# Graph attention on one core: value products on alternate column halves, and the denominators and degrees on four column groups of a bank of their own

## The chip, the cores and the metric

The kernel runs on one core of one Trainium2 chip. The metric is the device time of one execution in microseconds (us); lower is better.

## The reference, cut to what matters

Four graph layers run one after the other over 6,250 nodes of 64 features and 206,250 edges. Only the first, the attention layer, is touched by the change:

```python
def _L0_gnn_ref(x, edge_index, qk_w, qk_b, v_w, v_b, o_w, o_b, ln_g, ln_b):
    qk = x @ qk_w.T + qk_b
    v = x @ v_w.T + v_b
    src = edge_index[0]
    dst = edge_index[1]
    scores = jnp.sum(qk[dst] * qk[src], axis=-1) / math.sqrt(v.shape[-1])
    scores = jnp.clip(scores, -5.0, 5.0)
    seg_max = jax.ops.segment_max(scores, dst, num_segments=n)
    e = jnp.exp(scores - seg_max[dst])
    seg_sum = jax.ops.segment_sum(e, dst, num_segments=n)
    attn = e / seg_sum[dst]
    out = jax.ops.segment_sum(attn[:, None] * v[src], dst, num_segments=n)
    ...
```

The second layer needs the degree of each node, the number of edges that end in it, and takes it from the same pass.

## The kernel before, in words

The edges have been turned into a dense matrix of counts in DRAM (float16: how many edges lead from one node to another). The attention layer goes over this matrix as a dense one. Its columns, the receiving nodes, are cut into 13 **bands** (`NGRP`): the first, n = 0, has 352 columns (`GCOLS`, the last 128 nodes and 224 overflow columns), the other twelve 512. Its rows, the sending nodes, are 49 blocks of 128 (`NB`). One **iteration** i = 49 n + hi is one block of one band:

- `score(i)` (TensorE, L1185): the 128 x 512 scores, from 64 rows of `qT`, float32. Even iterations use array rows 0 to 63, odd ones rows 64 to 127. There are four banks for scores (`SB`, banks 0 to 3).
- `exp(i)` (ScalarE, L873): the exponential into `expo`, eight buffers (`EB`).
- `clip(i)` (VectorE, L1889) limits it to exp(-5) and exp(5), and `weigh_(i)` (VectorE, L1901) multiplies it by the counts in `chunkA` into `weighed`, eight buffers (`WB`). VectorE's order is written out: clip(i) always stands ahead of weigh_(i - 1), and at the end of a band too.
- `gain(i)` (TensorE, L1194): `vtab` times `weighed`, float32, added up over the 49 blocks in bank 4 or 5 (`SB + n % AB`). `vtab` has 66 columns: 64 values, a column of ones, whose product is the denominator (`seg_sum`), and a column of zeros.
- `degree(i)` (TensorE, L1202): 32 columns of `degw` times the counts themselves (float16) into the same bank, rows 64 to 95 and 96 to 127 in turn, which gives the degrees.

TensorE's order is written out as well, in **groups** of four iterations (`QUAD`): the scores of a group, then the gains and the degrees of the group before it, then what `between` adds. A band is twelve full groups and one of a single iteration (hi = 48):

```python
                    for i in now:
                        score(i)
                    for i in before_:
                        gain(i)
                    for i in before_:
                        degree(i)
                    for i in before_:
                        between(i)
                    before_ = now
```

`between` holds what belongs to a band's end. `att_fold(n)` (L1213) adds the overflow columns to a finished band with two products of 256 columns. ScalarE's `att_out(n)` (L881) copies the bank to `outT`. `att_back(n)` (L1222), at block 8 of the next band, turns it back to rows of nodes with four products against `mergeA` in bank 6, and VectorE's `att_sum` copies them to `sumsA`. Once, in band 1, the overflow columns are turned in the same way (L888, L1232, L1931).

SyncE loads `chunkA`, a ring of two buffers (`ARING`), four chunks to a band (`UCH`): three of 14 blocks (`CCH`) and one of 7. A load waits until the degrees of the chunk before the last are done (`att["used"]`).

Of the kernel before, what the change touches and what calls it, by code (L numbers as in the profile page):

```python
# [7 lines left out]
P = 128  # L8
N = 6250
D = 64  # L10
E = 206250
NB = -(-N // P)
# [39 lines left out]
DEGROW = 96  # L52
AR = DEGROW + 1
# [107 lines left out]
def build(nc, a, out):  # L161
    ctx = ExitStack()
    with ctx:
        def sb(name, shape, dt=F32):
            return ctx.enter_context(nc.sbuf_tensor(name, shape, dt))
# [131 lines left out]
        vtab = here("vtab", [P, NB, AC])  # L297
# [3 lines left out]
        outT = here("outT", [AR, 2, 512])  # L301
        foldA = here("foldA", [OV, 2, 256])
        overA = here("overA", [AR, 2 * OV])
# [3 lines left out]
        turnA = here("turnA", [D + 1, 2, GN * P])  # L307
# [3 lines left out]
        degw = here("degw", [P, 2, 32], F16)  # L311
# [518 lines left out]
        def _(act):  # L830
# [45 lines left out]
            def att_out(n):  # L876
                cols = 512 if n else P
                act.wait_ge(att["agg"], n + 1)
                if n >= 2:
                    act.wait_ge(att["back"], n - 1)  # L880
                nc.scalar.activation(outT[:, n % 2, 0:cols], bank[SB + n % AB][0:AR, 0:cols], ACT.Copy).then_inc(att["out"], 1)  # L881

            for i in range(NI):
                n, hi = divmod(i, NB)
                exp(i)
                if n == 1 and hi == 3:
                    act.wait_ge(att["used"], UCH)
                    nc.scalar.activation(overA[:, :], bank[SB][0:AR, OVC:GCOLS], ACT.Copy).then_inc(att["overturned"], 1)  # L888
                if n == 2 and hi == 0:
                    att_out(0)  # L890
                if n >= 2 and hi == 3:
                    att_out(n - 1)
# [140 lines left out]
        def _(pe):  # L1033
# [154 lines left out]
            def gain(i):  # L1188
                n, hi = divmod(i, NB)
                cols, to = 512 if n else GCOLS, bank[SB + n % AB]  # L1190
                pe.wait_ge(att["weighed"], i + 1)
                if hi == 0 and n >= AB:
                    pe.wait_ge(att["out"], n - AB + 1)
                nc.tensor.matmul(to[0:AC, 0:cols], vtab[:, hi, :], weighed[:, i % WB, 0:cols], start=hi == 0, stop=False,  # L1194
                                 skip_group_check=True).then_inc(att["gained"], 1)

            def degree(i):
                n, hi = divmod(i, NB)
                cols, to = 512 if n else GCOLS, bank[SB + n % AB]
                c, m = divmod(hi, CCH)  # L1200
                row = D + i % 2 * 32
                last = nc.tensor.matmul(to[row:row + 32, 0:cols], degw[:, i % 2, :], chunkA[:, (n * UCH + c) % ARING, 0:cols * CCH]  # L1202
                                        .rearrange("p (k c e) -> p k c e", c=CCH, e=BLK)[:, :, m, :],
                                        start=i % 2 == 1 and hi < 2, stop=False, skip_group_check=True)
                if hi % CCH == CCH - 1 or hi == NB - 1:
                    last.then_inc(att["used"], 1)

            def att_fold(n):
                cols, to = 512 if n else P, bank[SB + n % AB]
                pe.wait_ge(att["hot"], n + 1)  # L1210
                pe.wait_ge(att["overcopied"], 1)
                for d in range(2):
                    last = nc.tensor.matmul(to[0:AC, d:cols:2], overT[:, d, :], foldA[:, n % 2, 0:cols // 2], start=False, stop=d == 1,  # L1213
                                            skip_group_check=True)
                last.then_inc(att["agg"], 1)

            def att_back(n):
# [3 lines left out]
                for b in range(4 if n else 1):  # L1221
                    last = nc.tensor.matmul(bank[6][:, b * AC:(b + 1) * AC], outT[:, n % 2, b * P:(b + 1) * P], mergeA[0:AR, :],  # L1222
                                            start=True, stop=True)
# [3 lines left out]
            def between(i):  # L1227
                n, hi = divmod(i, NB)
                if n == 1 and hi == 8:
                    pe.wait_ge(att["overturned"], 1)  # L1230
                    for d in range(2):
                        last = nc.tensor.matmul(bank[7][0:OV, d * P:d * P + AC], overA[:, d:2 * OV:2], mergeA[0:AR, :],  # L1232
                                                start=True, stop=True)
# [11 lines left out]
            for n in range(NGRP + 1):  # L1245
                for first in range(0, NB if n < NGRP else 1, QUAD):
# [3 lines left out]
                    for i in before_:  # L1250
                        gain(i)
                    for i in before_:
                        degree(i)
# [285 lines left out]
        def _(v):  # L1539
# [291 lines left out]
            nc.vector.memset(vtab[:, :, D:AC], 0.0)  # L1831
            nc.vector.memset(degw[:, :, :], 0.0)
            link(nc.vector.tensor_copy(mergeA[:, :], ident[:, 0:AC]))
            link(nc.vector.memset(rowsA[:, :, :, :], 1.0))
            link(nc.vector.memset(vtab[:, :, D:D + 1], 1.0))
            link(nc.vector.memset(degw[:, 0, 1:2], 1.0))
            link(nc.vector.memset(degw[:, 1, 0:1], 1.0))
            link(nc.vector.memset(mergeA[DEGROW:DEGROW + 1, D + 1:AC], 1.0))
# [79 lines left out]
            for i in range(NI + 1):  # L1918
# [10 lines left out]
                if n == 1 and hi == 20:  # L1929
                    v.wait_ge(att["overturned"], 2)  # L1930
                    nc.vector.tensor_copy(overT[:, :, :], bank[7][0:OV, 0:2 * P].rearrange("p (d c) -> p d c", d=2)[:, :, 0:AC])\  # L1931
# [344 lines left out]
```

## Time and profile before

| what | value |
|---|---|
| median of 3 runs | 13652.0 us (13648.86 to 13652.0) |
| the profiled execution's own time | 13654.69 us |
| its span | 13653.0 us |
| granted TensorE clock, mean | 0.892 of full speed |
| TensorE busy (matmul) | 11057.9 us, 81% of the span |
| VectorE busy | 5587.9 us, 41% |
| ScalarE busy | 3529.7 us, 26% |
| GpSimd busy | 4391.0 us, 32% |

Spans of the profile are in microseconds from the start; a busy TensorE is the union of its matmuls. The trace shows every float32 product as two matmul instructions, here called its two passes, each with its own weight load (LDWEIGHTS, on the engine PEld); a float16 product is one. In a row, 64*128 means 64 active rows and 128 active columns of the array. The start of a row and the start of the next one give the time that a piece takes; the length in the row's second column reaches over the end of the last instruction and overlaps the next piece.

### The profile page before, as it was taken

What the parts mean: (1) busy time and instruction counts of PE and PEld (TensorE: products, weight loads), DVE (VectorE), ACT (ScalarE), POOL (GpSimd) and SP (SyncE); (2) the same over time, 40 slices, a digit from 0 to 9 for tenths busy, and PEclk for the clock granted to TensorE, in tenths of its full rate; (3) what the DMA queues carried; (4) which work ended last, traced back from release to release, by engine and by line L of the source; (5) the groups of instructions that cost most, each with busy time, mean ns of one, the idle gap of its engine ahead of it and who ended that gap; (6) DMA issues with size and microseconds to landing.
All of it is one profiled execution on the core that took longest, in us unless ns stands there. A gap on an engine that the chain in (4) does not pass through costs nothing.

```text
span 13653.0 us, 258090 instructions
## 1 busy us (share of the span) xinstructions
PE 11057.9 (81%) x60251; PEld 6361.4 (47%) x60252; DVE 5587.9 (41%) x21367; ACT 3529.7 (26%) x9549; POOL 4391.0 (32%) x3429
## 2 busy tenths in 40 slices
PE   2888888799976777777777777775899999999999
PEld 2444444333345555555555555554644444444443
DVE  6888888766624443443443443443311111111111
ACT  0666666533302222222222222222100000000000
POOL 2000000000005888888888888886000000000000
PEclk7666666699988999999999999998599999999999
DMA  2444444422262333333333333335399899899898
GB/s 99 139 136 139 139 136 140 139 87 93 87 273 36 42 42 42 42 42 42 42 42 42 42 42 42 42 42 35 109 354 348 338 348 348 337 349 348 338 349 306
DMA packets 1120492, 2096.55 MB, mean 154 GB/s; under 512 B 373090, under 2 KB 982915, under 8 KB 1012532
## 3 DMA queue, kind: packets, MB, share of 16 engines
q1 hardware_dynamic: 823768, 1913.47, 39.3%
q0 software_dynamic: 295904, 174.34, 12.0%
q8 instruction: 248, 4.06, 0.1%
q14 instruction: 572, 4.68, 0.1%
HBM read 1630.21 MB, written 457.17 MB: 153 GB/s over the span
## 4 chain that ended last, share of the span: by engine, by line
PE 54%; issue 19%; POOL 16%; DVE 4%; DMA 2%; ACT 1%; POOLq 1%; SPq 1%; DVEq 0%; ACTq 0%; another core or an unknown queue 0%
PE ps L1491 16%; PE ps L1139 11%; PE ps L1496 9%; POOL G L499 8%; POOL reverse L824 8%; PE ps L1194 4%; PE ps L1185 2%; DMA reverse<-SD,sidx 2%; DVE hots L1824 1%; PE ps L1294 1%; PE ps L1343 1%; PE ps L1354 1%; PE ps L1344 1%; POOLq L823 1%; PE ps L1357 1%
## 5 line engine op out<-in xcount | busy, mean ns | idle before, releaser
L824 POOL DMA_INDIRECT reverse<-SD,sidx x1660 | 2650.9, 1597 | 556.4 <-issue 496.2
L1491 PE MATMUL ps<-chunk,feat 128*128 128x512 f16 (+1 forms) x10192 | 2278.9, 375 | 14.8 <-DVE feat L2186 13.9
L499 POOL DMA_INDIRECT G<-h_table,idx x1660 | 1647.4, 992 | 1942.9 <-issue 1935.5
L1139 PE MATMUL ps<-hots 128*128 128x392 f16 x4859 | 1893.7, 449 | 428.4 <-issue 212.9
L1354 PE MATMUL ps<-MS,OH 128*128 128x128 f32 x3320 | 774.4, 316 | 1218.2 <-issue 811.9
L2023 DVE TENSOR_TENSOR acc<-acc,ps 128x132 f32 x1660 | 485.1, 292 | 3009.7 <-PE ps L1357 2958.5
L854 ACT ACTIVATE stagebuf<-ps 128x392 f32 x3248 | 1470.5, 506 | 884.5 <-PE ps L1142 804.8
L1491 PEld LDWEIGHTS ps<-chunk,feat 128*128 128x128 bf16 x10192 | 943.4, 98 | 1301.2 <-issue 307.8
L931 ACT ACTIVATE SD<-ps 128x129 f32<-128x129 f32 x1660 | 461.9, 278 | 3726.4 <-DMA reverse<-SD,sidx 3700.5
L1354 PEld LDWEIGHTS ps<-MS,OH 128*128 128x128 f32 x3320 | 542.8, 198 | 1771.6 <-issue 1748.7
L1343 PE MATMUL ps<-early,OT 128*128 128x256 f32 x3320 | 1081.3, 409 | 250.9 <-issue 225.8
L1496 PE MATMUL ps<-chunk,feat 128*64 128x512 f16 (+1 forms) x10192 | 1212.6, 377 | 0.0
L2122 DVE TENSOR_TENSOR summed<-ps,upper 64x512 f32<-64x512 f32 (+1 forms) x208 | 139.5, 671 | 2581.0 <-ACT upper L984 2580.9
L1824 DVE TENSOR_TENSOR hots<-count_hi,key_hi 128x588 f16<-128x588 f16 x2430 | 1112.5, 458 | 0.0
L1344 PE MATMUL ps<-big,OT 128*128 x3320 | 1044.0, 398 | 0.0
L1139 PEld LDWEIGHTS ps<-hots 128*128 128x128 f16 x4859 | 494.0, 102 | 987.4 <-issue 607.5
L1142 PE MATMUL ps<-zero 128*128 128x1 bf16 x4859 | 936.0, 193 | 0.0
L1822 DVE TENSOR_TENSOR hots<-count_lo,key_lo 128x256 f16<-128x256 f16 x2430 | 706.2, 291 | 387.4 <-PE ps L1142 338.5
L984 ACT ACTIVATE upper<-ps 64x512 f32<-64x512 f32 (+1 forms) x208 | 121.4, 584 | 2760.5 <-PE ps L1496 2760.4
L1496 PEld LDWEIGHTS ps<-chunk,feat 128*64 128x64 bf16 x10192 | 515.1, 109 | 655.9 <-issue 301.4
L1357 PE MATMUL ps<-MS,EQ 128*128 128x129 f32 x3320 | 811.2, 327 | 0.0
L811 POOL DMA_INDIRECT slot_rows<-first_table,slot_of x2 | 1.9, 954 | 2414.6 <-DMA first_table<-H 2414.3
(417 smaller groups left out, 14865.9 us busy)
## 6 DMA issues: line engine op xcount, KB each, us to landing
chunk<-adj SPq DMA_DIRECT2D x720, 1792.0 KB, 9.0
adj<-stagebuf SPq DMA_DIRECT2D x406, 784.0 KB, 5.3
chunkA<-adj SPq DMA_DIRECT2D x48, 1792.0 KB, 6.8
chunk<-adj SPq DMA_DIRECT2D x60, 1232.0 KB, 6.5
G<-in_edge SPq DMA_DIRECT2D x1660, 32.0 KB
G<-h_table,idx POOLq DMA_INDIRECT x1660
reverse<-SD,sidx POOLq DMA_INDIRECT x1660
reverse<-acc SPq DMA_DIRECT2D x4, 3225.0 KB, 20.0
```

Source lines behind the costliest of these rows:

```text
L499: nc.gpsimd.indirect_dma_start(G[:, j, 0:width], None, table, bass.IndirectOffsetOnAxis(idx[:, j:j + 1], 0))\
L824: nc.gpsimd.indirect_dma_start(reverse[j % R], bass.IndirectOffsetOnAxis(sidx[:, j:j + 1], 0), SD[:, j % R, :], None, compute_op=ALU.add). ...
L854: nc.scalar.activation(stagebuf[:, bass.ds(held["word"][j] >> ENDBITS, SLEN)].rearrange("p (x c) -> p x c", c=BLK)[:, :, 0:2], bank[j % 8] ...
L1139: nc.tensor.matmul(ps[:, bass.ds(window % 8 * 512, 2 * COMBS)], hots[:, j // HG % HRING, 0:P, j % HG], hots[:, j // HG % HRING, P:P + 2 * ...
L1142: nc.tensor.matmul(ps[:, bass.ds((window + 1) % 8 * 512, 1)], zero16[:, :], zero16[:, 0:1], start=True, stop=True, skip_group_check=True). ...
L1343: nc.tensor.matmul(bank[2 + j % 2][:, 0:2 * M], OT[:, j % 2, 0:P], w("edge"), start=True, stop=False)
L1344: nc.tensor.matmul(bank[2 + j % 2][:, 0:2 * M], OT[:, j % 2, P:2 * P], big[:, bass.ds(b * 2 * M, 2 * M)], start=False, stop=True).then_inc ...
L1354: nc.tensor.matmul(bank[6][:, 0:M], OH[:, j % HOT, :], MS[:, j % MR, 0:M], start=True, stop=True)
L1357: nc.tensor.matmul(bank[4 + j % 2][:, 0:RC], EQ[:, j % MR, :], MS[:, j % MR, M:M + RC], start=True, stop=True).then_inc(mes["seg"], 1)
L1491: nc.tensor.matmul(bank[k % 2][:, 0:cols], feat[0][:, hi, 0:2, :].rearrange("p a d -> p (a d)"), columns(chunk4, i % DRING, m, cols), star ...
L1496: last = nc.tensor.matmul(bank[k % 2][half:half + D, 0:cols], feat[0][:, hi, 2, :], columns(chunk4, i % DRING, m, cols), start=False, stop ...
L1824: nc.vector.tensor_tensor(hots[:, j, P + 2 * NB:P + 2 * COMBS, :], count_hi[:, 2 * NB:2 * COMBS, :], keys_of(key_hi, k, 2 * COMBS - 2 * NB ...
```

## The change

The gains multiply 64 columns only, and write rows 0 to 63 of the band's bank for even iterations and rows 64 to 127 for odd ones. The denominators get products of their own, `weight_sum`: 32 columns of `denw` (one of them ones) times `weighed`, float32. They go to another bank, 6 for band 0 and 7 for all others (`sums_bank`), on rows 0, 32, 64 or 96 by hi % 4. The degrees go to the same bank and the same four groups of rows. The fold is made twice (64 columns, and 2 columns in the bank of the sums), so are the turn back and ScalarE's copy of a finished band, and `mergeA` adds the two halves and the four groups up. `weight_sum` of a band waits for the copy of the band before, since from band 1 on all bands use bank 7. `att["gained"]`, on which VectorE's ring of `weighed` waits, is now raised by `weight_sum`. The setup ahead of the attention pass has one memset of `vtab` less and a few small instructions for `mergeA` and `denw`.

```diff
...
 NI = NB * 13
 QUAD = 4
 SB, EB, WB, AB, ARING = QUAD, 2 * QUAD, 2 * QUAD, 2, 2
-DEGROW = 96
-AR = DEGROW + 1
+SROWS = 32
 LOW, HIGH = math.exp(-5.0), math.exp(5.0)
 PARTS = 3
 PADDST = NPAD - 1
...
 def build(nc, a, out):
     ctx = ExitStack()
     with ctx:
+        def sums_bank(n):
+
+            return bank[7 if n else 6]
+
         def sb(name, shape, dt=F32):
             return ctx.enter_context(nc.sbuf_tensor(name, shape, dt))
 
...
 
         phase = ExitStack()
         qT = here("qT", [P, NPAD + 2 * OV])
-        vtab = here("vtab", [P, NB, AC])
+        vtab = here("vtab", [P, NB, D])
         chunkA = here("chunkA", [P, ARING, CHUNK], F16)
         expo = here("expo", [P, EB, 512])
         weighed = here("weighed", [P, WB, 512])
-        outT = here("outT", [AR, 2, 512])
+        outT = here("outT", [P, 2, 512])
         foldA = here("foldA", [OV, 2, 256])
-        overA = here("overA", [AR, 2 * OV])
+        overA = here("overA", [P, 2 * OV])
         overT = here("overT", [OV, 2, AC])
         sumsA = here("sumsA", [P, NB, AC])
         rowsA = here("rowsA", [P, 2, GN, D + 1])
-        turnA = here("turnA", [D + 1, 2, GN * P])
+        overS = rowsA[:, :, :, :].rearrange("p a b c -> p (a b c)")[:, 0:2 * OV]
+        turn_sum = here("turn_sum", [P, 2, GN * P])
+        turnA, sumT = turn_sum[0:D + 1, :, :], turn_sum[:, :, :]
         slot_rows = here("slot_rows", [P, 2, D])
         slot_of = here("slot_of", [P, 2], I32)
         slot_f = here("slot_f", [P, 2])
-        degw = here("degw", [P, 2, 32], F16)
+        degw = here("degw", [P, SROWS], F16)
+        denw = here("denw", [P, SROWS])
         mergeA = here("mergeA", [P, AC])
         phase.close()
 
...
                 act.wait_ge(att["agg"], n + 1)
                 if n >= 2:
                     act.wait_ge(att["back"], n - 1)
-                nc.scalar.activation(outT[:, n % 2, 0:cols], bank[SB + n % AB][0:AR, 0:cols], ACT.Copy).then_inc(att["out"], 1)
+                nc.scalar.activation(sumT[:, n % 2, 0:cols], sums_bank(n)[:, 0:cols], ACT.Copy)
+                nc.scalar.activation(outT[:, n % 2, 0:cols], bank[SB + n % AB][:, 0:cols], ACT.Copy).then_inc(att["out"], 1)
 
             for i in range(NI):
                 n, hi = divmod(i, NB)
                 exp(i)
                 if n == 1 and hi == 3:
                     act.wait_ge(att["used"], UCH)
-                    nc.scalar.activation(overA[:, :], bank[SB][0:AR, OVC:GCOLS], ACT.Copy).then_inc(att["overturned"], 1)
+                    nc.scalar.activation(overS, sums_bank(0)[:, OVC:GCOLS], ACT.Copy)
+                    nc.scalar.activation(overA[:, :], bank[SB][:, OVC:GCOLS], ACT.Copy).then_inc(att["overturned"], 1)
                 if n == 2 and hi == 0:
                     att_out(0)
                 if n >= 2 and hi == 3:
...
                 pe.wait_ge(att["weighed"], i + 1)
                 if hi == 0 and n >= AB:
                     pe.wait_ge(att["out"], n - AB + 1)
-                nc.tensor.matmul(to[0:AC, 0:cols], vtab[:, hi, :], weighed[:, i % WB, 0:cols], start=hi == 0, stop=False,
+                half = slice(D, P) if i % 2 else slice(0, D)
+                nc.tensor.matmul(to[half, 0:cols], vtab[:, hi, :], weighed[:, i % WB, 0:cols], start=hi < 2, stop=False,
+                                 skip_group_check=True)
+
+            def weight_sum(i):
+                n, hi = divmod(i, NB)
+                cols, row = 512 if n else GCOLS, hi % 4 * SROWS
+                if hi == 0 and n >= 2:
+                    pe.wait_ge(att["out"], n)
+                nc.tensor.matmul(sums_bank(n)[row:row + SROWS, 0:cols], denw[:, :], weighed[:, i % WB, 0:cols], start=hi < 4, stop=False,
                                  skip_group_check=True).then_inc(att["gained"], 1)
 
             def degree(i):
                 n, hi = divmod(i, NB)
-                cols, to = 512 if n else GCOLS, bank[SB + n % AB]
+                cols, row = 512 if n else GCOLS, hi % 4 * SROWS
                 c, m = divmod(hi, CCH)
-                row = D + i % 2 * 32
-                last = nc.tensor.matmul(to[row:row + 32, 0:cols], degw[:, i % 2, :], chunkA[:, (n * UCH + c) % ARING, 0:cols * CCH]
+                last = nc.tensor.matmul(sums_bank(n)[row:row + SROWS, 0:cols], degw[:, :],
+                                        chunkA[:, (n * UCH + c) % ARING, 0:cols * CCH]
                                         .rearrange("p (k c e) -> p k c e", c=CCH, e=BLK)[:, :, m, :],
-                                        start=i % 2 == 1 and hi < 2, stop=False, skip_group_check=True)
+                                        start=False, stop=False, skip_group_check=True)
                 if hi % CCH == CCH - 1 or hi == NB - 1:
                     last.then_inc(att["used"], 1)
 
...
                 pe.wait_ge(att["hot"], n + 1)
                 pe.wait_ge(att["overcopied"], 1)
                 for d in range(2):
-                    last = nc.tensor.matmul(to[0:AC, d:cols:2], overT[:, d, :], foldA[:, n % 2, 0:cols // 2], start=False, stop=d == 1,
-                                            skip_group_check=True)
+                    nc.tensor.matmul(to[0:D, d:cols:2], overT[:, d, 0:D], foldA[:, n % 2, 0:cols // 2], start=False, stop=d == 1,
+                                     skip_group_check=True)
+                for d in range(2):
+                    last = nc.tensor.matmul(sums_bank(n)[0:2, d:cols:2], overT[:, d, D:AC], foldA[:, n % 2, 0:cols // 2], start=False,
+                                            stop=d == 1, skip_group_check=True)
                 last.then_inc(att["agg"], 1)
 
             def att_back(n):
...
                 if n >= 1:
                     pe.wait_ge(att["summed"], n)
                 for b in range(4 if n else 1):
-                    last = nc.tensor.matmul(bank[6][:, b * AC:(b + 1) * AC], outT[:, n % 2, b * P:(b + 1) * P], mergeA[0:AR, :],
+                    nc.tensor.matmul(bank[6][:, b * AC:b * AC + D], outT[:, n % 2, b * P:(b + 1) * P], mergeA[:, 0:D],
+                                     start=True, stop=True)
+                    last = nc.tensor.matmul(bank[6][:, b * AC + D:(b + 1) * AC], sumT[:, n % 2, b * P:(b + 1) * P], mergeA[:, D:AC],
                                             start=True, stop=True)
                 last.then_inc(att["back"], 1)
 
...
                 if n == 1 and hi == 8:
                     pe.wait_ge(att["overturned"], 1)
                     for d in range(2):
-                        last = nc.tensor.matmul(bank[7][0:OV, d * P:d * P + AC], overA[:, d:2 * OV:2], mergeA[0:AR, :],
-                                                start=True, stop=True)
+                        to = GCOLS + d * AC
+                        nc.tensor.matmul(bank[SB][0:OV, to:to + D], overA[:, d:2 * OV:2], mergeA[:, 0:D],
+                                         start=False, stop=True, skip_group_check=True)
+                        last = nc.tensor.matmul(bank[SB][0:OV, to + D:to + AC], overS[:, d:2 * OV:2], mergeA[:, D:AC],
+                                                start=False, stop=True, skip_group_check=True)
                     last.then_inc(att["overturned"], 1)
                 if n >= 2 and hi == 8:
                     att_back(0 if n == 2 else n - 1)
...
                         score(i)
                     for i in before_:
                         gain(i)
+                    for i in before_:
+                        weight_sum(i)
                     for i in before_:
                         degree(i)
                     for i in before_:
...
 
             v.wait_ge(built, 1)
             v.wait_ge(x_loaded, 16)
-            nc.vector.memset(vtab[:, :, D:AC], 0.0)
-            nc.vector.memset(degw[:, :, :], 0.0)
-            link(nc.vector.tensor_copy(mergeA[:, :], ident[:, 0:AC]))
-            link(nc.vector.memset(rowsA[:, :, :, :], 1.0))
-            link(nc.vector.memset(vtab[:, :, D:D + 1], 1.0))
-            link(nc.vector.memset(degw[:, 0, 1:2], 1.0))
-            link(nc.vector.memset(degw[:, 1, 0:1], 1.0))
-            link(nc.vector.memset(mergeA[DEGROW:DEGROW + 1, D + 1:AC], 1.0))
+            nc.vector.memset(degw[:, :], 0.0)
+            nc.vector.memset(denw[:, :], 0.0)
+            nc.vector.tensor_tensor(mergeA[:, 0:D], ident[:, 0:D], ident[:, D:P], ALU.add)
+            link(nc.vector.tensor_copy(mergeA[:, D:AC], ident[:, 0:2]))
+            for q in range(1, P // SROWS):
+                link(nc.vector.tensor_tensor(mergeA[:, D:AC], mergeA[:, D:AC], ident[:, q * SROWS:q * SROWS + 2], ALU.add))
+            nc.vector.memset(rowsA[:, :, :, :], 1.0)
+            nc.vector.memset(denw[:, 0:1], 1.0)
+            link(nc.vector.memset(degw[:, 1:2], 1.0))
             nc.vector.tensor_scalar(slot_f[:, :], slot_at[:, 0, :], float(NPAD - 1), 0.0, ALU.min, ALU.max).then_inc(att["slots"], 1)
             v.wait_ge(att["slots"], 1)
             nc.vector.tensor_copy(slot_of[:, :], slot_f[:, :]).then_inc(att["slots"], 1)
...
                     att_hot(n)
                 if n == 1 and hi == 20:
                     v.wait_ge(att["overturned"], 2)
-                    nc.vector.tensor_copy(overT[:, :, :], bank[7][0:OV, 0:2 * P].rearrange("p (d c) -> p d c", d=2)[:, :, 0:AC])\
+                    nc.vector.tensor_copy(overT[:, :, :], bank[SB][0:OV, GCOLS:GCOLS + 2 * AC].rearrange("p (d c) -> p d c", d=2))\
                         .then_inc(att["overcopied"], 1)
                 if n >= 2 and hi == 12:
                     att_sum(0 if n == 2 else n - 1)
```

The order of TensorE at the end of band 1, before (`ps` is the PSUM, the shape is columns of the product's weights by columns streamed; L1194 is the gain, L1202 the degree, L1213 the fold):

```order
L1185 MATMUL ps<-qT 128x512
L1194 MATMUL ps<-weighed,vtab 66x512 x4
L1202 MATMUL ps<-chunkA,degw 32x512 x4
L1185 MATMUL ps<-qT 128x512 x4
L1194 MATMUL ps<-weighed,vtab 66x512
L1202 MATMUL ps<-chunkA,degw 32x512
L1213 MATMUL ps<-foldA,overT 66x64 x2
L1213 MATMUL ps<-foldA,overT 66x256 x2
L1185 MATMUL ps<-qT 128x512 x4
```

and with the change (L1193 is the score, L1203 the gain, L1211 `weight_sum`, L1218 the degree, L1230 and L1233 the two folds; line numbers are the changed kernel's):

```order
L1193 MATMUL ps<-qT 128x512
L1203 MATMUL ps<-weighed,vtab 64x512 x4
L1211 MATMUL ps<-weighed,denw 32x512 x4
L1218 MATMUL ps<-chunkA,degw 32x512 x4
L1193 MATMUL ps<-qT 128x512 x4
L1203 MATMUL ps<-weighed,vtab 64x512
L1211 MATMUL ps<-weighed,denw 32x512
L1218 MATMUL ps<-chunkA,degw 32x512
L1230 MATMUL ps<-foldA,overT 64x64 x2
L1233 MATMUL ps<-foldA,overT 2x64 x2
L1230 MATMUL ps<-foldA,overT 64x256 x2
L1233 MATMUL ps<-foldA,overT 2x256 x2
```

Nothing is reordered. A row of 32-column products stands between gains and degrees, and each fold has a second one of 2 columns behind it.

The order of TensorE where band 1 is turned back, in band 2, before:

```order
L1202 MATMUL ps<-chunkA,degw 32x512 x4
L1185 MATMUL ps<-qT 128x512 x4
L1194 MATMUL ps<-weighed,vtab 66x512 x4
L1202 MATMUL ps<-chunkA,degw 32x512 x4
L1222 MATMUL ps<-mergeA,outT 128x66 x4
L1185 MATMUL ps<-qT 128x512 x4
```

and with the change (of the last two rows, L1242 and L1244, each comes four times, in turn):

```order
L1193 MATMUL ps<-qT 128x512 x4
L1203 MATMUL ps<-weighed,vtab 64x512 x4
L1211 MATMUL ps<-weighed,denw 32x512 x4
L1218 MATMUL ps<-chunkA,degw 32x512 x4
L1242 MATMUL ps<-mergeA,outT 128x64
L1244 MATMUL ps<-mergeA,turn_sum 128x2
```

Each of the four products of 66 columns has become one of 64 and one of 2, with weights of 128 columns each (`outT`, and `turn_sum` for the sums).

## Rows read from the trace of the kernel before

**Rows 1.** The page, part 4: shares of the chain that ended last, by line.
```profile
PE ps L1491 16%; PE ps L1139 11%; PE ps L1496 9%; POOL G L499 8%; POOL reverse L824 8%; PE ps L1194 4%; PE ps L1185 2%; DMA reverse<-SD,sidx 2%; DVE hots L1824 1%; PE ps L1294 1%; PE ps L1343 1%; PE ps L1354 1%; PE ps L1344 1%; POOLq L823 1%; PE ps L1357 1%
```
**Rows 2.** Busy time by stretch: the columns, and one stretch of the attention pass.
```profile
core 0: us, PE busy (x) PEld busy (x) DVE busy (x) ACT busy (x) POOL busy (x), PEclk, DMA share, GB/s
...
2905.00:2980.00 75.00, 74.12 (x250) 23.12 (x247) 47.40 (x100) 25.98 (x50) 0.00 (x0) 1.00 0.26 99
```
**Rows 3.** Groups by line, 2750 to 3738 us: busy us, mean ns | idle before, releaser.
```profile
L1194 PE MATMUL ps<-weighed,vtab 128*66 128x512 f32 (+1 forms) x1274 | 570.4, 589 | 10.4 <-DVE weighed L1901 10.4
L1901 DVE TENSOR_TENSOR weighed<-expo,chunkA 128x512 f32<-128x512 f32 (+1 forms) x637 | 427.5, 671 | 0.1
L873 ACT ACTIVATE expo<-ps 128x512 f32<-128x512 f32 (+1 forms) x637 | 323.7, 593 | 629.8 <-PE ps L1185 629.8
...
L1889 DVE TENSOR_SCALAR expo<-expo 128x512 f32<-128x512 f32 (+1 forms) x637 | 264.3, 415 | 337.7 <-ACT expo L873 337.7
```
**Rows 4.** Timeline of TensorE, one full group: start us, us, engine, line, tiles, count.
```profile
3205.57 3.65 PE L1194 MATMUL ps<-weighed,vtab 128*66 128x512 f32 x8
3209.15 0.61 PE L1202 MATMUL ps<-chunkA,degw 128*32 128x512 f16 x4
3209.69 1.99 PE L1185 MATMUL ps<-qT 64*128 64x512 f32 x8
```
**Rows 5.** Timeline of all engines from the scores of a group on.
```profile
3203.66 1.99 PE L1185 MATMUL ps<-qT 64*128 64x512 f32 x8
...
3204.82 2.06 ACT L873 ACTIVATE expo<-ps 128x512 f32<-128x512 f32 x4 [3.97 <-PE ps L1185]
3205.45 0.43 DVE L1889 TENSOR_SCALAR expo<-expo 128x512 f32<-128x512 f32 x1 [2.20 <-ACT expo L873]
...
3205.79 0.68 DVE L1901 TENSOR_TENSOR weighed<-expo,chunkA 128x512 f32<-128x512 f32 x1
...
3206.39 0.42 DVE L1889 TENSOR_SCALAR expo<-expo 128x512 f32<-128x512 f32 x1
```
**Rows 6.** Timeline of TensorE, 3203.6 to 3203.8 us: what starts in it.
```profile
3203.66 0.70 PE L1185 MATMUL ps<-qT 64*128 64x512 f32 x2
```
**Rows 7.** Timeline of TensorE from the last product of a band on.
```profile
2953.84 1.12 PE L1185 MATMUL ps<-qT 64*128 64x512 f32 x2
2954.90 3.65 PE L1194 MATMUL ps<-weighed,vtab 128*66 128x512 f32 x8
...
2959.02 1.99 PE L1185 MATMUL ps<-qT 64*128 64x512 f32 x8
2961.88 1.07 PE L1194 MATMUL ps<-weighed,vtab 128*66 128x512 f32 x2 [0.88 <-DVE weighed L1901]
2962.89 0.39 PE L1202 MATMUL ps<-chunkA,degw 128*32 128x512 f16 x1
2963.21 1.08 PE L1213 MATMUL ps<-foldA,overT 112*66 112x256 f32 x4
2964.22 1.56 PE L1185 MATMUL ps<-qT 64*128 64x512 f32 x6
```
**Rows 8.** Timeline of TensorE where a band's sums are turned back.
```profile
2922.63 1.11 PE L1222 MATMUL ps<-mergeA,outT 97*128 97x66 f32 x8
2923.67 0.70 PE L1185 MATMUL ps<-qT 64*128 64x512 f32 x2
```
**Rows 9.** Timeline of TensorE, 2727.0 to 2728.5 us: products on two column halves.
```profile
2727.00 1.98 PE L1169 MATMUL ps<-turnA,early 65*64 65x512 f32 x4
```
**Rows 10.** Busy time by stretch, the stretch of rows 9.
```profile
2700.00:2750.00 50.00, 49.38 (x175) 29.55 (x173) 14.18 (x36) 7.26 (x12) 1.91 (x2) 0.50 0.13 48
```
**Rows 11.** Groups of TensorE by line, 3850 to 4100 us.
```profile
L1294 PE MATMUL ps<-chunk,feat_conv 128*128 128x512 f16 x588 | 135.5, 380 | 0.0
L1299 PE MATMUL ps<-chunk,feat_conv 128*64 128x512 f16 x588 | 73.9, 383 | 0.0
```
**Rows 12.** DMA issues of the attention pass: KB each, median us to landing.
```profile
chunkA<-adj SPq DMA_DIRECT2D x20, 1792.0 KB, 6.9
```

## The prediction

> **What bounds the kernel now.** The page's chain by line comes first: the products that the change touches are L1194 with 4% of the span, and L1185 with 2% beside them [rows 1]. Nearly all the rest lies elsewhere and is left as it is. The attention pass runs from about 2750 to 3740 us, some 990 us. The windows show TensorE busy for 74.1 of 75 us there, at a granted clock of 1.00 (the 2.4 GHz level); VectorE is busy for 47.4 and ScalarE for 26.0 [rows 2]. The groups by line say the same: exp waits 629.8 us for scores and clip 337.7 us for exp, while the gains wait 10.4 us [rows 3]. TensorE is the bound, and what is taken off it counts until VectorE is late.
>
> The timeline gives the price of each piece of a full group, from start to start [rows 4, 5]. The scores of four iterations take 3205.57 - 3203.66 = 1.91 us, the gains 3209.15 - 3205.57 = 3.58, the degrees 0.54; a group is 6.03 us. 
>
> **The change, part by part.**
>
> Gains on column halves. Two products would share a slot, as the scores do. For float32 rows 9 speak: two products of 512 columns on two column halves, four passes in all, took 1.98 us at the 1.2 GHz level [rows 9, 10]. A pass there costs twice 0.43, 0.86, so four in a row would be 3.4 us, and two slots are 1.7. For 128 rows and float16 another stage says it: 588 products over the full width were 135.5 us, 588 on halves 73.9 [rows 11]. So I take four slots, 1.72 + 0.14 = 1.86 us, for 3.58 before.
>
> A new wait there. VectorE puts clip(i) ahead of weigh_(i - 1), so the last weigh of a group waits for the first exp of the next. In rows 5 that weigh starts 2.13 us after the scores do (3205.79 against 3203.66) and takes 0.68: it ends at 2.81. Rows 7 show it as a stall: a lone gain started 2.86 after its scores (2961.88 against 2959.02). The second pair of gains would start at 1.91 + 0.05 + 0.86 = 2.82. It waits some 0.04 us: gains 1.90.
>
> `weight_sum`. Four products of 32 columns, float32, on four column groups. No row shows four groups side by side. The bounds are two slots (all four together), 0.86 + 0.05 = 0.91 us, and four slots (two together, all that [rows 9, 11] show), 1.77; serial, 3.5, is excluded by those rows. I take 0.91: row halves, column halves in float32 and in float16 and the two groups of the degrees all shared fully, and nothing in them hints at a limit of two. The Trainium skill has a figure for this, in "TensorE: Matmul & The Clock Gate", Part 3: three tiles of 32 columns gave 2.38 times. Estimated by it, slots are 0.43 x 3 / 2.38 = 0.54 us, and the time would be near 13590 us; no row here shows three or four tiles.
>
> Degrees. Four groups and the shape of `weight_sum`: one slot, 0.21 + 0.11 = 0.32 us, for 0.54.
>
> A full group is then 1.91 + 1.90 + 0.91 + 0.32 = 5.04 us for 6.03: **0.99 saved**. Is VectorE in time? Its clips start 0.94 us apart (3205.45, 3206.39) [rows 5], so four iterations are 3.76 us, under 5.04. ScalarE needs 2.06. The first weigh of a group is done after about 3.7 us, its gain comes at 5.04 + 1.91. `weight_sum` raises `gained` a period before VectorE's ring of eight needs it. Both are covered by over a microsecond; only the last weigh is tight.
>
> Band's end [rows 7]. The period that begins with the lone scores was 2959.02 - 2953.84 = 5.18 us. Now its second pair of gains waits until 2.86: 2.86 + 0.86 + 0.09 = 3.81, then 0.91 + 0.32, in all 5.04; 0.14 saved. The next period was 2964.22 - 2959.02 = 5.20: the stall to 2.86, the lone gain 1.01, its degree 0.32, the fold 1.01. The stall stays. A lone `weight_sum` adds 0.91, and the second fold, again four passes of 256 columns, 1.01: 1.92 lost. Turning back took 2923.67 - 2922.63 = 1.04 us for eight passes [rows 8]; now there are sixteen. Their streams are 64 and 2 columns, but each loads weights of 128 columns, so I double it: 1.04 lost (0.3 if short streams help).
>
> ScalarE copies twice. The copy was one instruction, the new one as wide, 0.6 us like an exp [rows 3]. It starts once the fold ends, when the next scores begin, and the first exp follows these by 1.16 us (3204.82 - 3203.66): 1.2 beside 1.16, next to nothing. `weight_sum` of the new band waits for this copy; it comes 1.9 + 1.9 us after the fold, so bank 7 alone is enough.
>
> DMA. The tightest load is that of a band's first chunk: freed by the degrees of block 41, and needed two periods and about 3 us later, 5.04 + 3.1 = 8.1 us, about as before (5.18 + 3.1). Loads take 6.9 [rows 12]. It stays hidden, by about 1 us.
>
> Setup. VectorE's list loses a memset of `vtab` and two short ones, and gains about four small instructions: nothing.
>
> **The sum.** A 512-column band has eleven full periods: 11 x 0.99 = 10.9, + 0.14 - 1.92 - 1.04 = 8.1 us saved. Twelve bands: 97. Band 0 has 352 columns; 0.99 x 352/512 = 0.68 at most for a group, less since exp, clip and weigh shrink more slowly than the slots. Taken as 0.5: 11 x 0.5 = 5.5. Its own fold and turn back cost about 1.5 more. In all **101 us**. From the profiled execution's 13654.7 (1.7 over its span, 2.7 over the median of the runs): 13554. Against the median, 13652 - 101 = **13551 us**, 0.74% less. This kernel's runs lie within 3 us; 0.2%, 27 us, is about what a measurement can tell from no change.
>
> **The rivals.**
>
> Two groups at a time, so that the change ends *slower*. The array streams at most two products of 128 rows side by side, whatever the number of groups: four float32 streams ask for twice what any row has shown. `weight_sum` takes 1.77, the degrees 0.54; a group is 6.12, 0.09 over before. Bands: 11 x 0.09 + (6.12 - 5.18) + 1.92 + 1.04 = 4.9 us lost, x 12 = 59, and some 4 for band 0: 13715. The saving of the gains (1.7 us a group) is handed to `weight_sum`. It turns at 0.99 - 8.1/11 = 0.25 us saved a group: above 5.78 us the kernel is slower. For it: no row has four groups. Against: nothing shows two to be a limit.
>
> A part of it. Four streams run at three quarters: slots of 0.57, `weight_sum` 1.19, degrees 0.39, a group 5.39. Per band 11 x 0.64 - 0.2 - 1.92 - 1.04 = 3.9 saved; 13652 - 47 - 3 = 13602. A last weigh that comes 0.3 us later in each group gives about the same (11 x 12 x 0.3 = 40 us).
>
> In program order. If products started strictly in order, product 1 could not start before product 0's second pass, and four products would take five slots: gains 2.29, `weight_sum` 2.20, a group 6.72. Per band 11 x 0.69 + 1.3 + 1.92 + 1.04 = 11.9 lost: 13795. Rows 6 speak against it, since two products start together there. The same page of the Trainium skill, in its Part 3, says that matmuls keep program order in start and end. By that rule this rival would be the case; the trace does not agree, since both first passes start within rows 6's 0.2 us, and I go by the trace.
>
> It does not do what it says: column halves with 128 rows and float32 don't share. Gains stay at 3.58, a group is 6.72, and the time is near 13790. Rows 9 (float32, 65 rows) and 11 (128 rows, float16) each exclude half of it.
>
> **How the numbers follow.** Forecast 0.66: every kind of sharing in the trace is complete. A part of it 0.16. Two at a time 0.10. Program order 0.03, no sharing 0.03, anything else 0.02. The forecast's own bounds: down by a cheap turn back (0.7 x 12 = 8), no tight weigh (5), a cheaper second fold (6) and smaller costs between shapes (12), to 13520; up through the partial case, to 13620, together 0.82. Faster by over 0.2%: 0.66 and nearly all of the partial case, 0.80. Within it 0.04, from a partial case with slots near 0.7 us. Slower 0.16.
>
> **What would show it.** In the profile after: TensorE's timeline with groups of 5.0 us; eight passes of `weight_sum` in 0.9; four degrees in 0.3; a short stall on `weighed` in each group; second folds of 1.0, turns back of 2.1; the attention pass some 100 us shorter, all else unmoved. I am wrong if `weight_sum` takes 1.8 or more, if gains with 64 columns stay near 3.6, or if idle time ahead of them, put down to `weighed`, passes 0.3 us a group.

## The result, and the profile after

The changed kernel takes 13563.3 us (median, 13560.5 to 13571.4) against 13652.0 us before (13648.9 to 13658.5), four runs each: a ratio of 0.9935, with a 95% interval of 0.9922 to 0.9947. It is 88.7 us faster; 101 were forecast, and the time lies inside the forecast's range of 13520 to 13620 us.

The profiled execution took 13563.1 us. Its attention pass, from the first score to the start of the last turn back, is read from the first and last starts of two lines:

```profile
L1193 PE MATMUL ps<-qT x1274: 456/589/950, 2748.7 to 3639.6; 64*128 64x512 f32 x168, 64*128 64x352 f32 x14
```

(the scores) and

```profile
L1242 PE MATMUL ps<-mergeA,outT x98: 275/288/323, 2887.3 to 3651.1; 128*128 128x64 f32 x98
```

(the turns back). That is 3651.1 - 2748.7 = 902.4 us. Before, L1185 began at 2749.6 and the last turn back (L1222) at 3740.9: 991.3. The pass is 89 us shorter, which is the whole of what the runs show; what lies outside it differs by some 3 us between the two profiles.

The groups of instructions of the pass, from 2750 to 3650 us, the counterpart of [rows 3]:

```profile
L1929 DVE TENSOR_TENSOR weighed<-expo,chunkA 128x512 f32<-128x512 f32 (+1 forms) x637 | 429.2, 674 | 0.0
L1203 PE MATMUL ps<-weighed,vtab 128*64 128x512 f32 (+1 forms) x1274 | 345.6, 601 | 10.5 <-DVE weighed L1929 10.4
L879 ACT ACTIVATE expo<-ps 128x512 f32<-128x512 f32 (+1 forms) x637 | 323.7, 592 | 512.2 <-PE ps L1193 512.2
...
L1917 DVE TENSOR_SCALAR expo<-expo 128x512 f32<-128x512 f32 (+1 forms) x637 | 265.6, 417 | 247.6 <-ACT expo L879 247.5
L1211 PE MATMUL ps<-weighed,denw 128*32 128x512 f32 (+1 forms) x1274 | 176.3, 594 | 0.0
...
L1218 PE MATMUL ps<-chunkA,degw 128*32 128x512 f16 (+1 forms) x637 | 66.3, 374 | 0.0
```

The passes of the gains and of the denominators together keep TensorE busy for 345.6 + 176.3 = 521.9 us, where the gains alone had 570.4. ScalarE waits less for scores (512.2 us for 629.8). TensorE is still the bound, as [rows 2] had it; VectorE's share rose from 47.4 to 51.3 of 75 us:

```profile
2905.00:2980.00 75.00, 74.12 (x388) 23.77 (x389) 51.27 (x109) 28.43 (x55) 0.00 (x0) 1.00 0.26 99
```

TensorE's timeline over one full group, the counterpart of [rows 4, 5]:

```profile
3204.31 1.99 PE L1193 MATMUL ps<-qT 64*128 64x512 f32 x8
3206.23 2.03 PE L1203 MATMUL ps<-weighed,vtab 128*64 128x512 f32 x8
3208.18 1.07 PE L1211 MATMUL ps<-weighed,denw 128*32 128x512 f32 x8
3209.07 0.40 PE L1218 MATMUL ps<-chunkA,degw 128*32 128x512 f16 x4
3209.39 1.99 PE L1193 MATMUL ps<-qT 64*128 64x512 f32 x8
```

From start to start: scores 1.92 us, gains 1.95, `weight_sum` 0.89, degrees 0.32; in all 3209.39 - 3204.31 = 5.08 us for 6.03. The end of a band, the counterpart of [rows 7]:

```profile
2931.55 1.12 PE L1193 MATMUL ps<-qT 64*128 64x512 f32 x2
2932.60 2.89 PE L1203 MATMUL ps<-weighed,vtab 128*64 128x512 f32 x8
...
2936.63 1.99 PE L1193 MATMUL ps<-qT 64*128 64x512 f32 x8
2939.50 1.07 PE L1203 MATMUL ps<-weighed,vtab 128*64 128x512 f32 x2 [0.88 <-DVE weighed L1929]
2940.51 1.04 PE L1211 MATMUL ps<-weighed,denw 128*32 128x512 f32 x2
2941.39 0.38 PE L1218 MATMUL ps<-chunkA,degw 128*32 128x512 f16 x1
2941.70 1.08 PE L1230 MATMUL ps<-foldA,overT 112*64 112x256 f32 x4
2942.71 1.02 PE L1233 MATMUL ps<-foldA,overT 112*2 112x256 f32 x4
2943.66 1.56 PE L1193 MATMUL ps<-qT 64*128 64x512 f32 x6
```

The period that begins with the lone scores is 5.08 us (5.18 before), the next one 2943.66 - 2936.63 = 7.03 (5.20 before), the second fold 0.95 of it. Where the band is turned back, the counterpart of [rows 8] (the two kinds of products alternate, four times each):

```profile
2958.92 0.43 PE L1242 MATMUL ps<-mergeA,outT 128*128 128x64 f32 x2
2959.19 0.34 PE L1244 MATMUL ps<-mergeA,turn_sum 128*128 128x2 f32 x2
...
2960.80 1.99 PE L1193 MATMUL ps<-qT 64*128 64x512 f32 x8
```

It takes 2960.80 - 2958.92 = 1.88 us for 1.04. Here is what was not foreseen, in the timeline of all engines right behind it:

```profile
2960.91 0.43 DVE L1943 COPY sumsA<-ps 128x264 f32<-128x264 f32 x1 [3.32 <-PE ps L1244]
...
2962.72 2.82 PE L1203 MATMUL ps<-weighed,vtab 128*64 128x512 f32 x8
...
2964.46 0.19 PEld L1203 LDWEIGHTS ps<-weighed,vtab 128*64 128x64 f32 x2 [0.70 <-DVE weighed L1929]
...
2965.47 1.06 PE L1211 MATMUL ps<-weighed,denw 128*32 128x512 f32 x8
```

VectorE stood still for 3.32 us, until the turn back was done, ahead of its copy to `sumsA`. The gains of that group then took 2965.47 - 2962.72 = 2.75 us and not 1.95, because weights of theirs waited for `weighed`. In the kernel before, VectorE stood still at the same place just as long:

```profile
2923.77 0.43 DVE L1915 COPY sumsA<-ps 128x264 f32<-128x264 f32 x1 [3.43 <-PE ps L1222]
```

but the gains behind its turns back took 3.58 us like all others.

### The profile page after: what moved, and what is told of

Read it like the earlier page. It is cut to its first block, busy times and chain, and to the rows that moved or that the text cites. A ratio compares the mean times of both kernels' runs of the same rounds, so it can differ in the third digit from the quotient of the medians.

```text
span 13561.3 us, 260962 instructions
## 1 busy us (share of the span) xinstructions
PE 10980.6 (81%) x61679; PEld 6352.3 (47%) x61680; DVE 5577.2 (41%) x21369; ACT 3538.1 (26%) x9563; POOL 4391.2 (32%) x3429
## 4 chain that ended last, share of the span: by engine, by line
PE 51%; issue 16%; POOL 13%; DMA 11%; DVE 4%; ACT 2%; SPq 1%; POOLq 0%; DVEq 0%; ACTq 0%
PE ps L1518 16%; PE ps L1147 11%; DMA reverse<-SD,sidx 11%; PE ps L1523 9%; POOL G L505 7%; POOL reverse L830 5%; PE ps L1203 2%; PE ps L1193 2%; DVE hots L1851 1%; PE ps L1211 1%; PE ps L1321 1%; ACT SD L939 1%; ACT stagebuf L860 1%; PE ps L1460 1%; PE ps L1326 1%
```

## The experiments

Unless the text says otherwise, each is an edit of the changed kernel, and the pass is measured in the trace as above, with starts to the nanosecond: before 991.3 us, changed kernel 902.4. A second measurement of the changed kernel (e10) gave 902.3, so a difference of a microsecond in it can be read. Times of different experiments can't be set side by side: the kernel before took 13652.6 us beside e1 to e3, 13666.6 beside e4 to e7 and 13665.2 beside e8 to e11. What counts is the ratio to it, and the pass.

**e1 and e2: fewer column groups for the denominators.** The degrees keep their four groups of rows.

```diff
-                cols, row = 512 if n else GCOLS, hi % 4 * SROWS
+                cols, row = 512 if n else GCOLS, hi % 2 * SROWS
...
-                nc.tensor.matmul(sums_bank(n)[row:row + SROWS, 0:cols], denw[:, :], weighed[:, i % WB, 0:cols], start=hi < 4, stop=False,
+                nc.tensor.matmul(sums_bank(n)[row:row + SROWS, 0:cols], denw[:, :], weighed[:, i % WB, 0:cols], start=hi < 2, stop=False,
...
-                                        start=False, stop=False, skip_group_check=True)
+                                        start=2 <= hi < 4, stop=False, skip_group_check=True)
```

(e2 has 1 for each of these 2.)

> The changed kernel with the denominators' products on two column groups (rows 0 and 32) in place of four. Theory (as many groups as there are share the array fully): weight_sum of a full group goes from two slots to four, 0.88 + 2 x 0.43 = 1.74 us, and the period from 5.09 to 5.95 us; 156 full groups, 144 of them 512 columns wide (0.86 each) and 12 of 352 (0.59 each): 131 us more than the changed kernel, about 13694 us. Rival (the number of groups isn't what makes weight_sum short, for instance because its weights of 32 columns load fast): weight_sum stays near 0.9 us, and the time near 13563.

> The same with all denominators' products on one column group (rows 0 to 31). Theory: eight passes one behind the other, 8 x 0.43 + 0.02 = 3.46 us for 0.88; with the first experiment this gives three points, 0.88, 1.74 and 3.46 us for four, two and one group. 144 x 2.58 + 12 x 1.77 = 393 us more than the changed kernel, about 13956. Rival (the array takes up only two products at a time however many groups there are, and four products on two groups already cost what one group costs): e1 would then be near 1.74 by another reason and e2 the same as e1.

Measured, in one run each: 13691.0 and 13947.0 us; the passes 1031.1 and 1291.4 us, 128.7 and 389.0 longer than the changed kernel's, for 131 and 393 expected. One group of e1, from its `weight_sum` on:

```profile
3205.18 1.05 PE L1211 MATMUL ps<-weighed,denw 128*32 128x512 f32 x4
3205.65 0.39 PE L1218 MATMUL ps<-chunkA,degw 128*32 128x512 f16 x2
3206.07 1.03 PE L1211 MATMUL ps<-weighed,denw 128*32 128x512 f32 x4
3206.93 0.39 PE L1218 MATMUL ps<-chunkA,degw 128*32 128x512 f16 x2
3207.24 1.13 PE L1193 MATMUL ps<-qT 64*128 64x512 f32 x4
```

and of e2:

```profile
3206.59 2.76 PE L1211 MATMUL ps<-weighed,denw 128*32 128x512 f32 x6
3208.77 0.40 PE L1218 MATMUL ps<-chunkA,degw 128*32 128x512 f16 x3
3209.19 1.02 PE L1211 MATMUL ps<-weighed,denw 128*32 128x512 f32 x2
3210.05 0.38 PE L1218 MATMUL ps<-chunkA,degw 128*32 128x512 f16 x1
3210.36 1.12 PE L1193 MATMUL ps<-qT 64*128 64x512 f32 x2
```

Only the last row of degrees adds to the time; those before it start while passes of `weight_sum` are still under way. From the first pass of `weight_sum` to that last row it is 0.89 us on four groups (3209.07 - 3208.18 above), 1.75 on two and 3.46 on one. Twice the groups is half the time, up to four: the theory stands. The rival that the array takes two at a time is out, and so is the one that the narrow weights make `weight_sum` short: they are the same in all three kernels.

**e3: without the products of the denominators.** This kernel leaves out the sums of the weights.

```diff
-                    for i in before_:
-                        weight_sum(i)
...
-            link(nc.vector.memset(degw[:, 1:2], 1.0))
+            link(nc.vector.memset(degw[:, 0:2], 1.0))
```

> The changed kernel without the denominators' products: weight_sum is left out, att[gained] is raised by the gains, the degrees open the four groups, and their column 0 is one as well, so that the denominators are the edge counts and no sums of weights. Theory (TensorE stays the bound): a full group loses 0.88 us and comes to 4.2 us, still above VectorE's 3.77; the lone one at a band's end loses 0.88 too. 157 x 0.88 for bands of 512 and 0.62 for band 0 gives 12 x 13 x 0.88 + 13 x 0.62 = 145 us less than the changed kernel, near 13418. Rival (VectorE is close behind and its order of clip ahead of weigh makes the last gain late): the stall ahead of the last gain grows, a group is 4.4 or more, and under 115 us are saved.

Measured: 13419.8 us, ratio 0.9829 (0.9812 to 0.9845) to the kernel before; the pass 757.9 us, 144.5 shorter than the changed kernel's, for 145 expected. Its full groups:

```profile
3210.06 1.99 PE L1193 MATMUL ps<-qT 64*128 64x512 f32 x8
3211.97 2.02 PE L1203 MATMUL ps<-weighed,vtab 128*64 128x512 f32 x8
3213.93 0.40 PE L1212 MATMUL ps<-chunkA,degw 128*32 128x512 f16 x4
3214.26 1.99 PE L1193 MATMUL ps<-qT 64*128 64x512 f32 x8
```

A group is 3214.26 - 3210.06 = 4.20 us, and the gains stay at 1.96. So the change is a large gain and a large price: halves and four-group degrees (with the second fold, the second turn back and all else kept) take 991.3 - 757.9 = 233.4 us off the pass, and the denominators' own products put 144.5 back.

**e4: VectorE's copy of a band later.**

```diff
-                if n >= 2 and hi == 12:
+                if n >= 2 and hi == 15:
...
-                if n == 2 and hi == 24:
+                if n == 2 and hi == 27:
```

> The changed kernel with VectorE's copy of a turned-back band (att_sum) three iterations later: behind weigh of block 15 in place of 12 (and 27 for 24 in band 2). Theory (VectorE, which stands still for 3.3 us until the turn back is done, then lacks the lead for the group it is in, and TensorE waits 0.8 us on it): the gains of that group go from 2.75 back to 1.96 us, eleven or twelve times 0.79: 9 us less than the changed kernel, near 13554. Rival (the 0.8 us come from the longer turn back itself, or from ScalarE's second copy): they stay, and the time near 13563.

Measured: the pass 893.4 us, 9.0 shorter, as expected. The scores and gains behind a turn back:

```profile
2962.70 1.99 PE L1193 MATMUL ps<-qT 64*128 64x512 f32 x8
2964.61 2.02 PE L1203 MATMUL ps<-weighed,vtab 128*64 128x512 f32 x8
2966.57 1.06 PE L1211 MATMUL ps<-weighed,denw 128*32 128x512 f32 x8
```

The gains are 2966.57 - 2964.61 = 1.96 us; the stall is gone, though the turn back takes as long as before. By runs alone (13561.5 us, 0.9924, 0.9911 to 0.9938) it can't be told from the changed kernel; the trace tells it.

**e5: the last weigh of a group ahead of the next group's first clip.**

```diff
+                ahead = i and i % NB % QUAD == 0
+                if ahead:
+                    weigh_(i - 1)
                 if i < NI:
                     clip(i)
                 if i == 0:
                     continue
-                weigh_(i - 1)
+                if not ahead:
+                    weigh_(i - 1)
```

> The changed kernel with VectorE's order turned round at each group's first iteration: weigh of the group before's last iteration ahead of the clip of the new group's first. Theory (that clip waits for scores that TensorE makes after the gains could have started): gains of a full group go from 1.96 to 1.86 us (132 x 0.10 = 13 us; in band 0 from 1.57 to 1.3, 3 us), the stall of 0.95 us ahead of a band's lone gain and that of 0.86 ahead of the last pair of a band's full groups go (12 x 1.8 = 22 us): 38 us less than the changed kernel, near 13525. Rival (the last weigh is late because VectorE has no lead, whatever its order): under 10 us.

Measured: 13539.8 us, ratio 0.9908 (0.9893 to 0.9923); the pass 862.5 us, 39.9 shorter, for 38 expected. The intervals of the ratios just touch (the changed kernel's starts at 0.9922); the pass tells them apart. A full group:

```profile
3212.45 1.94 PE L1203 MATMUL ps<-weighed,vtab 128*64 128x512 f32 x8
3214.32 1.07 PE L1211 MATMUL ps<-weighed,denw 128*32 128x512 f32 x8
3215.20 0.40 PE L1218 MATMUL ps<-chunkA,degw 128*32 128x512 f16 x4
3215.53 1.99 PE L1193 MATMUL ps<-qT 64*128 64x512 f32 x8
```

The gains take 1.87 us: 0.09 us of each group was the wait for the last weigh. Behind a turn back they take 2.42 us for 2.75, so this order gives back part of that stall too.

**e6: the two products of a fold on two column groups.**

```diff
-                    nc.tensor.matmul(to[0:D, d:cols:2], overT[:, d, 0:D], foldA[:, n % 2, 0:cols // 2], start=False, stop=d == 1,
+                    nc.tensor.matmul(to[d * D:(d + 1) * D, d:cols:2], overT[:, d, 0:D], foldA[:, n % 2, 0:cols // 2], start=False, stop=d == 1,
...
-                    last = nc.tensor.matmul(sums_bank(n)[0:2, d:cols:2], overT[:, d, D:AC], foldA[:, n % 2, 0:cols // 2], start=False,
+                    last = nc.tensor.matmul(sums_bank(n)[d * SROWS:d * SROWS + 2, d:cols:2], overT[:, d, D:AC], foldA[:, n % 2, 0:cols // 2], start=False,
```

> The changed kernel with the two products of each fold on different column groups (odd columns of the band onto rows 64 to 127, and onto rows 32 and 33 of the bank of sums). Theory (products on different column groups share the array here as well): the folds go from 1.01 and 0.96 us to some 0.58 and 0.53, 13 times 0.86: 11 us less than the changed kernel, near 13552. Rival (the fold's strided output or the change of shape sets its time): nothing.

Measured: the pass 892.7 us, 9.7 shorter, for 11 expected. Its folds:

```profile
2946.16 0.65 PE L1230 MATMUL ps<-foldA,overT 112*64 112x256 f32 x4
2946.75 0.60 PE L1233 MATMUL ps<-foldA,overT 112*2 112x256 f32 x4
2947.28 1.99 PE L1193 MATMUL ps<-qT 64*128 64x512 f32 x8
```

They take 0.59 and 0.53 us for 1.01 and 0.95. By runs alone (13570.1 us, 0.9930, 0.9916 to 0.9944) it is not told apart either. Nothing but the place of the output differs here, so it is the two column groups that make the products share the array; their width is what it was.

**e7 and e11: all three.**

> The three before together. Theory (the three costs are apart from each other): 9 + 38 + 11 = 58 us less than the changed kernel, near 13505. Rival (they overlap: with weigh ahead, VectorE has the lead that the late copy gave it, so the first of the three adds nothing): near 13514.

Measured: 13525.5 us, ratio 0.9898 (0.9882 to 0.9913); the pass 846.1 us, 56.3 shorter, near what the parts sum to (9.0 + 39.9 + 9.7 = 58.6). They are not quite apart: e5 alone had taken 0.33 of the stall's 0.79 us. The rival that they overlap wholly (39.9 + 9.7 = 49.6 us) is out. This kernel and the changed one were run once more, on one chip:

> The changed kernel once more, for a comparison with e11 on the same chip: a ratio of 0.9935 to the kernel before, as in the first measurement, and an attention pass of 902 us.

> The kernel of e7 once more, on the chip of e10. Its attention pass was 846 us against the 902 us of the changed kernel; if that is all, it is 56 us below e10.

Measured: 13577.7 us (0.9936, 0.9923 to 0.9950) and 13521.0 us (0.9893, 0.9878 to 0.9908), the kernel before at 13665.2. The difference is 56.7 us, the traces' 902.3 - 846.2 = 56.1. It is the fastest kernel of the study that computes the whole result.

**e8 and e9: the same two edits of VectorE's order in the kernel before.**

> The kernel before with the turned-round order of weigh and clip of e5. Theory (the order was free in full groups before, since the last gain of a group started 1.7 us after its weigh was done, and cost only the stall of 0.95 us ahead of a band's lone gain): 12 x 0.95 + 1.3 for band 0's = 13 us less than the kernel before, in the attention pass; full groups stay at 6.04 us. Rival (the order cost the same 38 to 40 us before as it does in the changed kernel): 40 us less.

> The kernel before with the later att_sum of e4. Theory (before, VectorE stood still just as long for the turn back, but no gain waited for it, with 6.04 us for a group of which VectorE uses 3.77): no change, the attention pass at 991 us. Rival (the stall was there before too): 9 us less.

Measured: e8 13653.8 us, ratio 0.9993 (0.9983 to 1.0002), pass 980.2 us, 11.2 shorter than the kernel before's, for 13 expected; e9 13666.5 us, ratio 1.0001 (0.9992 to 1.0010), pass 991.0 us, as before. Neither is told from the kernel before by its runs; the pass tells e8. Its full groups stay at 6.03 us, and only the stall ahead of the lone gain goes:

```profile
2961.75 1.99 PE L1185 MATMUL ps<-qT 64*128 64x512 f32 x8
2963.67 1.07 PE L1194 MATMUL ps<-weighed,vtab 128*66 128x512 f32 x2
```

that gain starts 1.92 us after its scores, for 2.86 [rows 7]. At 6.03 us a group the two orders cost 11.2 us and nothing; at 5.08 they cost 39.9 and 9.0.

## Why the prediction was right, and where it was off

- **TensorE is the bound, and full groups carry the gain.** Right: 5.08 us for 6.03, 0.95 saved where 0.99 was forecast.
- **Gains on halves share fully** (from a float32 row with 65 rows and a float16 one). Right: without the late weigh they take 1.87 us (e5), 1.86 was the sum. That it is the halves, and not 64 columns for 66, rests on two things: passes stand 0.43 us apart with 66 columns in the kernel before and with 32 on one group in e2 (3.46 us for eight), so the width doesn't change a pass's time; and e6 moved nothing but the output.
- **`weight_sum` in two slots.** Right: 0.89 us, 0.91 forecast. It was the choice with the least behind it, since no row had four groups. e1 and e2 show that no limit sets in before four. The term was taken for the right reason, that sharing in the trace was complete wherever it occurred, but that was argued then and is shown only now.
- **A tight last weigh.** Right in kind, off in size: 0.09 us (e5) for 0.04. The wait was put together from rounded starts of two rows; over 132 full groups of the wide bands, the 0.04 us by which a group is longer than forecast came to some 5 us.
- **Band's end.** 5.08 and 7.03 us for 5.04 and 7.12 forecast; the turn back 1.88 for 2.08, since the 2-column products (0.20 us) are cheaper than the 64-column ones (0.25).
- **"Only the last weigh is tight."** Wrong, and the largest miss: 9.0 us (e4). The prediction gave VectorE's lead as over a microsecond and did not ask where VectorE itself waits. Its order has the copy of a turned-back band behind weigh 12, and TensorE makes the turn back only after the degrees of blocks 8 to 11. VectorE stood still for it before as well (3.43 us, and 3.32 now), but no gain waited then (e9: no effect there).
- **VectorE's order.** The stall of 0.95 us ahead of a lone gain was read from [rows 7] and taken as a given. e8 shows that it is a matter of order, worth 11.2 us in the kernel before. In the changed one the same order costs 3.1 us in a wide band: 0.95 ahead of the lone gain, 0.95 in the gains before it (2.82 us above, from 2932.60 to 2935.42, for 1.87), 0.09 in each of ten other groups, and 0.33 behind the turn back.
- **ScalarE's second copy and the loads.** Right: in the profile after no product of the denominators waits for the copy, and none for `chunkA`, whose loads take 6.7 us.

The balance: per wide band 11 x 0.95 = 10.4, + 0.10 - 1.83 (7.03 for 5.20) - 0.84 (the turn back) - 0.79 (the stall) = 7.1 us. The two traces say the same from one band's first score to the next one's: nine bands gave 7.0 or 7.1 us each, 63.4 in all; band 0 gave 5.8, band 1, in which nothing is turned back, 9.6, band 2, in which the sums of two bands are turned back, 6.2, and the last one, up to its own turn back, 4.1. Together that is the pass's 89. From 101 to 89: some 5 for the full groups, 9 for the stall, less 3 for the cheaper ends; under 1 us is left unexplained.

The rivals. Two groups at a time: excluded by e1 and e2. A part of it: excluded too, eight passes on four groups take 0.89 us, where it had 1.19, and two slots are 0.86. In program order: excluded by the gains' 1.95 us, where it had 2.29. No sharing: likewise, where it had 3.58.

## What to carry to other kernels

Where products of few columns bind TensorE, spread them over as many column groups as their width allows: here products of 32 columns in float32 cost a quarter each on four groups. But price the products that the narrower shape splits off: the 65th and 66th column cost nothing as part of a wide product (a pass takes 0.43 us with 66 columns and with 32), and 144 us as products of their own. And when the bound engine becomes faster, look for the waits of the other engines that used to end in its slack: two orders of VectorE's list that cost 11 us and nothing before cost 40 and 9 after.

## What the runs showed of the hardware beyond that

- Four streams of float32, each of 128 rows and 512 columns, ran side by side at the rate of one: eight passes in 0.89 us on four groups, 1.75 on two, 3.46 on one, at a granted clock of 1.00 in all three.
- Products overtake each other. In e2 the program has four products of the denominators, all on column group 0, and then four degrees, on groups 0 to 3. Its timeline above shows six passes, three degrees, two passes, one degree: three degrees started ahead of the last denominator's two passes, though they stand behind it in the program. That they are those of the free groups 1 to 3 fits, but the trace doesn't name the group. The Trainium skill says in "TensorE: Matmul & The Clock Gate", Part 3, that matmuls keep program order in start and end; for starts, this trace does not agree.
- A float32 product of 2 columns against weights of 128 columns took 0.20 us, one of 64 columns 0.25 us, from start to start in the turn back: a product that streams almost nothing still cost four fifths. What that floor consists of, the load of the weights or something else, no run here separates.
